# Pre-activation pair network on one core: the float16 high part of the normalised input from a second product instead of a cast

## The chip, the core and the metric

The kernel runs on one core of a Trainium2 chip. The metric is the device time of one execution in microseconds, as the median of repeated runs. The core has TensorE (PE, matmuls), VectorE (DVE), ScalarE (ACT), GpSimd (POOL) and the DMA queue of SyncE (SP), each with an instruction stream of its own. They meet through semaphores: an instruction may add to one when it is done, and an engine may wait until one has reached a value. Inputs and outputs lie in HBM, working data in SBUF (128 partitions), and matmuls write to PSUM, 8 banks of 512 float32 columns per partition.

## What is computed

x has the shape (1, 256, 256, 64). A group norm over 32 channel pairs is followed by a first layer that adds to x, then the same again with a second layer. The first layer begins with a layer norm over the channels, and that is the part the change touches:

```python
def _ln(x, w, b):
    mu = jnp.mean(x, axis=-1, keepdims=True)
    var = jnp.var(x, axis=-1, keepdims=True)
    return (x - mu) * jax.lax.rsqrt(var + EPS) * w + b
zn = _ln(z, ln_in_w, ln_in_b)
a = m * jax.nn.sigmoid(zn @ w_ag + b_ag) * (zn @ w_ap + b_ap)
b = m * jax.nn.sigmoid(zn @ w_bg + b_bg) * (zn @ w_bp + b_bp)
p = jnp.einsum('bikc,bjkc->bijc', a, b)
x = _ln(p, ln_out_w, ln_out_b) @ w_z + b_z
g = jax.nn.sigmoid(zn @ w_g + b_g)
return x * g
```

The second layer has gates, projections and a product of the same kind, with a norm over the whole tensor.

## The kernel before

All of x stays in SBUF, transposed, in the tensor XT_ALL (XT is a view of it): 64 groups of four image rows, 128 x 512 float32 each. The projections run as float16 matmuls in three terms, so each group of the normalised input is kept as a float16 high part, half(n, 0), and a float16 low part, half(n, 1), which together take the place of the group's float32 values in XT_ALL.

Stages, in order: load and transpose with the group statistics (to 60 us), the layer norm (60 to 236 us), gates and projections with the channel-wise products of the first layer (to about 500 us), the end of the first layer, then the second layer in the same way. The change lies in the layer norm.

The layer norm takes the 64 groups in four rounds of TG = 16, numbered t = 0 to 3. Two things run against each other:

- PE and ACT compute the variances, in the order of the function round_. For each group PE multiplies with a centring matrix (into banks 0 to 3), ACT writes the centred values back to XT_ALL (L844) and their squares to sq (L849), and PE adds the squares up into bank 4. Each of the two float32 matmuls of a group stands as two records.
- DVE, in normalise, turns the variances of a round into reciprocal spreads, split into three bfloat16 parts (parts3, L1232 to L1246). ACT's root (L835) is in the middle of it. Then for each group a small bfloat16 matmul of PE, spread_rstd, broadcasts the reciprocal spread to a bank, 5 or 6 in turn, DVE multiplies the centred group with that bank into one of eight slots of zn in float32 (L1258), and one group later casts the slot to float16 into half(n, 0) (L1279, in high). POOL subtracts the high part from the slot, which gives half(n, 1) (L997).

The spreads of round t-1 are put into PE's stream during the variance work of round t: from its sixth step on, two and one per step in turn (the order within a step: centring matmul, sum of the squares of the group before, spreads). A spread waits on zn_done until the product that last read its bank is done. PE runs its stream strictly in order, and so a spread that waits holds the variance work behind it. The next round's variances go to bank 4 only after DVE has read the old ones in L1232, by way of ACT, whose root comes ahead of its centring work.

The last round, t = 3, has no variance work beside it. There ACT makes the high parts (L862), DVE makes every third low part (L1274) and POOL the others.

DVE's product waits for bc_done (the spread is there) and lo_done (the slot's user of eight groups back, lo_done of n - 7, is done).

Of the kernel before, what the change touches and what calls it, by code (L numbers as in the profile page):

```python
# [37 lines left out]
GR = 4  # L38
# [19 lines left out]
TG = 16  # L58
NT = NG // TG
# [29 lines left out]
def build(nc, x, mask, w0, w1, bias0, bias1, vecs, consts, norm_consts, spread, ones3, out):  # L89
# [4 lines left out]
    ALU = mybir.AluOpType  # L94
    ACT = mybir.ActivationFunctionType
    ds = bass.ds
# [9 lines left out]
    with ctx:  # L106
# [3 lines left out]
        def sem(name):  # L110
            return ctx.enter_context(nc.semaphore(name))
# [3 lines left out]
        XT = XT_ALL[:, :].rearrange("p (r n) -> p r n", n=P)  # L115
# [16 lines left out]
        PS = ctx.enter_context(nc.psum_tensor("PS", [P, 8, BANK], f32))  # L132
# [4 lines left out]
        def half(g, i):  # L137

            return halves[:, ds(g * (2 * BANK) + i * BANK, BANK)]
# [32 lines left out]
        zn = xs.rearrange("p s r m -> p (s r m)")[:, 0:8 * BANK].rearrange("p (s n) -> p s n", s=8)  # L172
# [67 lines left out]
        hi_done = sem("hi_done")  # L240
# [13 lines left out]
        zn_done = sem("zn_done")  # L254
# [54 lines left out]
        def new_x_bank(g):  # L309

            return g % 2 + (0 if isinstance(g, int) and g >= NG - 2 else 2)
# [4 lines left out]
        def low_count(u):  # L316

            return NG - TG + sum(v not in LOWS_V for v in range(u + 1))
# [33 lines left out]
        def reached(eng, semaphore, value):  # L352

            if not isinstance(value, int) or value > 0:
                eng.wait_ge(semaphore, value)
# [136 lines left out]
        def _(pe):  # L492
            def mm(dst, lhsT, rhs, start=True, stop=True):
                return nc.tensor.matmul(dst, lhsT, rhs, start=start, stop=stop)  # L494
# [19 lines left out]
            for q in range(2):  # L514
                for h in range(2):
                    src = maskn.rearrange("p (h c q) -> p h q c", h=2, q=2)[:, h, q]
                    last = nc.tensor.transpose(PS[:, 7, (2 * q + h) * P:(2 * q + h + 1) * P], src, ident)
# [38 lines left out]
            def spread_rstd(t, u):  # L556

                if u == 0:
                    pe.wait_ge(rb_ready, t + 1)

                reached(pe, zn_done, t * TG + max(u - 1, 0))
                mm(PS[:, 5 + u % 2, :], spread_sb[:, u * P:(u + 1) * P], parts3).then_inc(bc_done, 1)


# [1 line left out]
            def round_(t):  # L566
                spread = 0
                for u in range(TG + 1):
                    if u < TG:
                        reached(pe, sq_ready, t * TG + (u - 3))  # L570
                        mm(PS[:, u % 4, :], cs, XT[:, ds(t * (TG * GR) + u * GR, GR), :].rearrange("p r n -> p (r n)")
                           ).then_inc(mm1_done, 1)
                    if u >= 1:
                        v = u - 1
                        pe.wait_ge(sq_ready, t * TG + (v + 1))
                        if v == 0:

                            reached(pe, var_ready, t + 1)
                        s0 = L_SEL + 30 - 2 * v
                        mm(PS[0:96, 4, :], NCF[:, s0:s0 + 96], sq[:, v % 2], v == 0, v == TG - 1).then_inc(mm2_done, 1)  # L580
                    if isinstance(t, int) and t == 0:
                        if u == SPREAD_LAG:
                            fold_weights()
                        if u == 2 * SPREAD_LAG:

                            small([(PS[:, 7, P:2 * P], ones, diag),
                                   (PS[:, 7, 2 * P:2 * P + 1], out_sq, ones[:, 0:1])])
                    elif SPREAD_LAG <= u < TG:
                        for _ in range(1 if (u - SPREAD_LAG) % 2 or u == TG - 1 else 2):
                            spread_rstd(t - 1, spread)  # L590
                            spread += 1
                assert spread in (0, TG)

            rounds(pe, round_, NT, 2)
            for layer in range(2):
# [113 lines left out]
                if layer == 0:  # L709
                    for u in range(TG):  # L710
                        spread_rstd(NT - 1, u)
                    pe.wait_ge(lo_done, low_count(TG - 1))
                    pe.wait_ge(lo_done_v, len(LOWS_V))
                else:

                    pe.wait_ge(biases_ready, 1)
                    for n in range(AP):
                        add_bias(0, n, False).then_inc(proj_done[1], 1)
# [3 lines left out]
                if layer == 1:  # L722
# [5 lines left out]
                    for step in range(NG + 2):  # L728
# [12 lines left out]
                        if 0 <= g < NG:  # L741
                            pe.wait_ge(o_done, g + 1)
                            reached(pe, ob_ready, g - 1)
                            for r in range(GR):
                                last = nc.tensor.transpose(PS[:, 6 + g % 2, r * P:(r + 1) * P],  # L745
                                                           x1sum[:, g % 4, r:BANK:GR], ident)
# [6 lines left out]
                for step in range(NG + 3):  # L753
                    g = step
                    if g < NG:
# [3 lines left out]
                        for r in range(GR):  # L759
                            last = nc.tensor.transpose(PS[:, 4 + g % 2, r * P:(r + 1) * P], pn[:, g % 2, r, :], ident)  # L760
# [6 lines left out]
                    if 0 <= g < NG:  # L767
# [5 lines left out]
                        for r in range(GR):  # L773
                            last = mm(bank[:, r * P:(r + 1) * P], pt[:, g % 2, r * P:(r + 1) * P], w_out,
                                      False, r == GR - 1)
                        last.then_inc(z_done, 1)
                    g = step - 3
                    if 0 <= g < NG:
# [11 lines left out]
                        for r in range(GR):  # L790
                            row = g * GR + r
                            last = nc.tensor.transpose(PS[:, new_x_bank(g), r * P:(r + 1) * P],  # L792
                                                       xb[:, row // HR % HS, row % HR, :], ident)
# [284 lines left out]
        def _(dve):  # L1078
# [17 lines left out]
            V = nc.vector  # L1096
# [132 lines left out]
            def normalise(t, last=False):  # L1229

                dve.wait_ge(mm2_done, t * TG + TG)
                V.tensor_scalar(ve[0:96, :], PS[0:96, 4, :], EPS, None, ALU.add).then_inc(var_ready, 1)  # L1232
                dve.wait_ge(std_ready, t + 2)
                r, w = rt[0:96, :], tmp[0:96, :]
                chain(t, V.reciprocal(r, sd[0:96, :]))
                chain(t, V.scalar_tensor_tensor(w, r, -0.5, r, ALU.mult, ALU.mult))
                chain(t, V.tensor_tensor(w, w, ve[0:96, :], ALU.mult))
                chain(t, V.scalar_tensor_tensor(r, w, 1.5, r, ALU.add, ALU.mult))

                reached(dve, bc_done, t * TG)  # L1240
                chain(t, V.tensor_copy(parts3[0:96, :], r))
                chain(t, V.tensor_tensor(r, r, parts3[0:96, :], ALU.subtract))
                chain(t, V.tensor_copy(parts3[32:64, :], r[32:64, :]))
                chain(t, V.tensor_copy(parts3[64:96, :], r[64:96, :]))
                chain(t, V.tensor_tensor(r[64:96, :], r[64:96, :], parts3[64:96, :], ALU.subtract))
                V.tensor_copy(parts3[64:96, :], r[64:96, :]).then_inc(rb_ready, 1)  # L1246
                for u in range(TG):
                    n = t * TG + u
                    dve.wait_ge(bc_done, n + 1)

                    if last and u >= 8:
                        if u - 8 in LOWS_V:
                            dve.wait_ge(lo_done_v, LOWS_V.index(u - 8) + 1)
                        else:
                            dve.wait_ge(lo_done, low_count(u - 8))
                    else:
                        reached(dve, lo_done, n - 7)
                    V.tensor_tensor(zn[:, u % 8], XT[:, ds(n * GR, GR), :].rearrange("p r n -> p (r n)"),  # L1258
                                    PS[:, 5 + u % 2, :], ALU.mult).then_inc(zn_done, 1)
                    if not last:  # L1260
                        if u > 0:
                            high(n - 1, (u - 1) % 8)
                    elif u - 2 in LOWS_V:
                        low(u - 2)
                if not last:
                    high(t * TG + TG - 1, (TG - 1) % 8)
                else:
                    assert LOWS_V[-1] < TG - 2

            def low(u):  # L1270

                n = NG - TG + u
                dve.wait_ge(hi_done, n + 1)
                V.tensor_tensor(half(n, 1), zn[:, u % 8], half(n, 0), ALU.subtract).then_inc(lo_done_v, 1)  # L1274

            def high(n, slot):

                dve.wait_ge(zn_done, n + 1)
                V.tensor_copy(half(n, 0), zn[:, slot]).then_inc(hi_done, 1)  # L1279

            CHAIN = 9
            made = [0]
# [1 line left out]
            def chain(t, ins):  # L1284

                made[0] += 1
                ins.then_inc(dve_chain, 1)
                dve.wait_ge(dve_chain, t * CHAIN + made[0])

            def normalise_round(t, last=False):  # L1290
                made[0] = 0
                normalise(t, last)
                assert made[0] == CHAIN
# [295 lines left out]
```

## Time and profile before

| | us |
|---|---|
| median of 3 runs | 1127.15 |
| lowest, highest | 1126.86, 1130.52 |
| profiled execution, device time | 1127.89 |
| profiled execution, span of the core | 1126.1 |
| PE, DVE, ACT, POOL busy in the span | 1005.5, 868.8, 688.3, 526.2 |

The span runs from the core's first to its last instruction; the device time has 1.8 us around it. Busy shares over the whole span hide the stages: in the layer norm the engines wait for each other in another pattern than later. Timelines give the start and the duration of an instruction, and in brackets how long its engine idled ahead of it and who ended that.

### The profile page before, as it was taken

The page shows a single profiled execution, that of the slowest core. Times are in us where ns is not written, and L with a number is a line of the kernel's source. Part 1 is how long each engine was busy: PE and PEld are TensorE (multiplying, and loading weights), DVE is VectorE, ACT ScalarE, POOL GpSimd, SP SyncE. Part 2 cuts the span into 40 slices and gives each one's busy share as a digit, 9 for nine tenths or more (in the row PEclk, how much of TensorE's full clock was granted, in tenths as well). Part 3 has the DMA queues.
Part 4 walks back from the last instruction along what each step waited for, and adds up shares of the span by engine and source line. Part 5 has one row for each costly group of instructions (what it writes and reads, how often), then busy time and mean ns, then how long its engine had stood idle before and what let it go on. Part 6 is the DMA issues. An engine that isn't in the chain of part 4 may idle for free.

```text
span 1126.1 us, 36346 instructions
## 1 busy us (share of the span) xinstructions
PE 1005.5 (89%) x14204; PEld 784.8 (70%) x14204; DVE 868.8 (77%) x1302; ACT 688.3 (61%) x1102; POOL 526.2 (47%) x447
## 2 busy tenths in 40 slices
PE   5699798579999999978999994989989898879997
PEld 5543333268898888968999994768777786645554
DVE  6817988966876868678888887866848678479997
ACT  5757565455656556565776672766847667546664
POOL 0001554586190734606777771542716437045553
PEclk9989999779999999998999996989999999989999
DMA  9800000000302112079989920003040130499995
GB/s 350 305 10 0 0 1 0 1 2 19 135 4 113 41 65 89 22 217 263 209 193 200 202 49 1 4 29 126 4 135 20 52 102 3 150 186 281 267 273 188
DMA packets 173196, 121.32 MB, mean 108 GB/s; under 512 B 69764, under 2 KB 152068, under 8 KB 173064
## 3 DMA queue, kind: packets, MB, share of 16 engines
q1 hardware_dynamic: 173064, 119.34, 39.8%
q8 instruction: 110, 1.80, 0.7%
q14 instruction: 22, 0.18, 0.1%
HBM read 68.99 MB, written 50.33 MB: 106 GB/s over the span
## 4 chain that ended last, share of the span: by engine, by line
PE 58%; DVE 16%; issue 11%; ACT 4%; DMA 4%; POOL 3%; DVEq 1%; SPq 1%; ACTq 0%; POOLq 0%
PE PS L494 53%; DVE WK L1399 4%; DMA AB<-x 3%; PE PS L760 3%; ACT WK L874 2%; PE PS L792 2%; DVE AB L1329 1%; DVE AB L1258 1%; DVE WK L1320 1%; POOL XT_ALL L997 1%; DVE AB L1325 1%; POOL AB L1058 1%; POOL AB L349 1%; DVE XT_ALL L1279 1%; DMA AB<-k_scratch 1%
## 5 line engine op out<-in xcount | busy, mean ns | idle before, releaser
L494 PE MATMUL PS<-EFF,XT_ALL 64*128 64x64 f16 (+1 forms) x10368 | 343.6, 201 | 8.7 <-POOL XT_ALL L997 3.6
L494 PEld LDWEIGHTS PS<-EFF,XT_ALL 64*128 64x128 f16 (+1 forms) x10368 | 316.4, 97 | 42.4 <-issue 16.4
L494 PE MATMUL PS<-AB 128*128 128x256 f16 (+3 forms) x1482 | 298.6, 355 | 41.8 <-POOL AB L1058 11.8
L494 PEld LDWEIGHTS PS<-AB 128*128 128x128 f16 (+3 forms) x1482 | 204.7, 140 | 133.6 <-issue 38.1
L874 ACT ACTIVATE WK<-PS,T 128x512 f32<-128x512 f32 x256 | 171.1, 683 | 94.9 <-PE PS L494 69.1
L1058 POOL TENSOR_TENSOR AB<-WK,AB 128x512 f32 x96 | 122.3, 1276 | 152.7 <-ACT AB L884 151.2
L349 POOL TENSOR_TENSOR AB<-WK,MS 128x512 f32 x96 | 130.6, 1388 | 105.6 <-DVE WK L1315 105.5
L997 POOL TENSOR_TENSOR XT_ALL<-AB,XT_ALL 128x512 f32 (+1 forms) x59 | 69.8, 1191 | 165.2 <-DVE XT_ALL L1279 154.9
L1068 POOL TENSOR_TENSOR WK<-XT_ALL 128x512 f32 (+1 forms) x64 | 73.8, 1155 | 85.3 <-PE PS L745 58.4
L1315 DVE TENSOR_TENSOR WK<-PS,WK 128x512 f32<-128x512 f32 x128 | 86.8, 689 | 31.2 <-ACT WK L874 24.9
L1320 DVE TENSOR_TENSOR WK<-PS,WK 128x512 f32<-128x512 f32 x128 | 87.3, 685 | 22.4 <-ACT WK L874 22.4
L1347 DVE BATCH_NORM_STATS2 REC<-WK 128x512 f32 x64 | 44.4, 694 | 61.6 <-ACT WK L906 61.6
L1403 DVE SCALAR_TENSOR_TENSOR WK<-WK,T 128x512 f32<-128x512 f32 x64 | 74.8, 1169 | 7.8 <-DVE WK L1399 2.0
L928 ACT ACTIVATE WK<-PS,T 128x512 f32<-128x512 f32 x64 | 49.4, 777 | 50.8 <-PE PS L494 50.8
L844 ACT ACTIVATE XT_ALL<-PS,T,CF 128x512 f32<-128x512 f32 (+1 forms) x64 | 49.7, 776 | 48.6 <-PE PS L494 48.6
L906 ACT ACTIVATE WK<-PS,T 128x512 f32<-128x512 f32 x64 | 44.0, 688 | 57.0 <-PE PS L494 56.2
L913 ACT ACTIVATE WK<-PS 128x512 f32<-128x512 f32 x64 | 41.1, 642 | 47.3 <-PE PS L494 45.6
L884 ACT ACTIVATE AB<-WK 128x512 f32 (+1 forms) x96 | 60.5, 630 | 15.4 <-DVE WK L1320 14.7
L494 PEld LDWEIGHTS PS<-EFF,WK 128*128 128x128 f32 x512 | 68.6, 195 | 1.9
L1342 DVE TENSOR_TENSOR S<-S,WK 128x512 f32<-128x512 f32 x64 | 44.6, 698 | 32.0 <-ACT WK L913 31.0
L494 PE MATMUL PS<-AB,EFF 128*128 128x512 f32 x128 | 66.7, 606 | 2.5 <-DMA AB<-k_scratch 2.5
L494 PE MATMUL PS<-EFF,WK 128*128 128x128 f32 x512 | 68.7, 278 | 0.0
(194 smaller groups left out, 1593.8 us busy)
## 6 DMA issues: line engine op xcount, KB each, us to landing
AB<-x SPq DMA_DIRECT2D x64, 512.0 KB, 7.0
p_scratch<-WK SPq DMA_DIRECT2D x32, 512.0 KB, 2.6
k_scratch<-WK SPq DMA_DIRECT2D x64, 256.0 KB, 2.1
AB<-k_scratch SPq DMA_DIRECT2D x32, 512.0 KB, 11.4
out<-AB SPq DMA_DIRECT2D x16, 1024.0 KB, 11.4
AB<-p_scratch SPq DMA_DIRECT2D x29, 512.0 KB, 7.6
AB<-p_scratch SPq DMA_DIRECT2D x2, 640.0 KB, 6.4
RAW<-w SPq DMA_DIRECT2D x2, 256.0 KB, 2.6
```

The costliest lines, as they stand in the source:

```text
L349: return eng.tensor_tensor(ab[:, :, :, ds(n4 * (4 * PR) + u * PR, PR)], sig[:, u], rows.unsqueeze(2).to_broadcast([P, 2, 2 * CHUNK, PR]), ...
L494: return nc.tensor.matmul(dst, lhsT, rhs, start=start, stop=stop)
L844: nc.scalar.activation(XT[:, ds(n * GR, GR), :].rearrange("p r n -> p (r n)"), PS[:, u % 4, :], ACT.Identity, bias=T[:, 15:16], scale=CF[: ...
L874: nc.scalar.activation(sig[:, u % 4], unit(layer, u)[:, :, 0:2 * CHUNK, :], ACT.Sigmoid, scale=T[:, 22:23] if layer == 0 else T[:, 28:29]) ...
L884: nc.scalar.activation(ab_hi[:, :, :, ds(n8 * (UB * PR) + u * PR, PR)], sig[:, u % 4], ACT.Copy).then_inc(abhi_done, 1)
L928: nc.scalar.activation(gate1[:, k % 4], PS[:, k % 4, :], ACT.Sigmoid, bias=T[:, 32:33], scale=T[:, 28:29]).then_inc(gate1_ready, 1)
L997: nc.gpsimd.tensor_tensor(half(n, 1), zn[:, u % 8], half(n, 0), ALU.subtract).then_inc(lo_done, 1)
L1058: nc.gpsimd.tensor_tensor(ab_rows(ab_lo, n4, u), sig[:, u], ab_rows(ab_hi, n4, u), ALU.subtract).then_inc(ablo_done, 1)
L1068: nc.gpsimd.tensor_tensor(x1sum[:, k % 4], half(g, 0), half(g, 1), ALU.add).then_inc(x1sum_done, 1)
L1315: V.tensor_tensor(gate, lin, gate, ALU.mult).then_inc(prod_done[0], 1)
L1320: V.tensor_tensor(gate, lin, gate, ALU.mult).then_inc(prod_done[1], 1)
L1403: V.scalar_tensor_tensor(x1sum[:, k % 4], x1sum[:, k % 4], col(24), gate1[:, k % 4], ALU.mult, ALU.add).then_inc(o_done, 1)
```

## The change

In the rounds t = 0 to 2 the helper high is gone. In its place DVE runs the product of L1258 a second time, directly after the first, with the same two inputs (the centred group in XT_ALL and the spread in PSUM) and with half(n, 0), float16, as its output; it adds to hi_done. It writes over the front half of the group that it reads. The bank of a spread is now read by two instructions, so that a later spread into it waits on hi_done instead of zn_done, except from the third spread of the last round on.

```diff
@@ spread_rstd (PE)
-                reached(pe, zn_done, t * TG + max(u - 1, 0))
+                if isinstance(t, int) and t == NT - 1 and u >= 2:
+                    pe.wait_ge(zn_done, t * TG + u - 1)
+                else:
+                    reached(pe, hi_done, t * TG + max(u - 1, 0))
                 mm(PS[:, 5 + u % 2, :], spread_sb[:, u * P:(u + 1) * P], parts3).then_inc(bc_done, 1)
@@ normalise (DVE)
                     V.tensor_tensor(zn[:, u % 8], XT[:, ds(n * GR, GR), :].rearrange("p r n -> p (r n)"),
                                     PS[:, 5 + u % 2, :], ALU.mult).then_inc(zn_done, 1)
                     if not last:
-                        if u > 0:
-                            high(n - 1, (u - 1) % 8)
+                        V.tensor_tensor(half(n, 0), XT[:, ds(n * GR, GR), :].rearrange("p r n -> p (r n)"),
+                                        PS[:, 5 + u % 2, :], ALU.mult).then_inc(hi_done, 1)
                     elif u - 2 in LOWS_V:
                         low(u - 2)
-                if not last:
-                    high(t * TG + TG - 1, (TG - 1) % 8)
-                else:
+                if last:
                     assert LOWS_V[-1] < TG - 2
-            def high(n, slot):
-
-                dve.wait_ge(zn_done, n + 1)
-                V.tensor_copy(half(n, 0), zn[:, slot]).then_inc(hi_done, 1)
```

On DVE, at the start of the groups of round 0, this stood there (AB holds parts3 and zn, PS is PSUM; line, operation, output, inputs, the semaphores waited for):

```order
L1245 TENSOR_TENSOR AB<-AB 32x512 [waits dve_chain]
L1246 CAST AB<-AB 32x512 [waits dve_chain]
L1258 TENSOR_TENSOR AB<-XT_ALL,PS 128x512 [waits bc_done] x2
L1279 CAST XT_ALL<-AB 128x512 [waits zn_done]
L1258 TENSOR_TENSOR AB<-XT_ALL,PS 128x512 [waits bc_done]
```

and at the same place stands now:

```order
L1248 TENSOR_TENSOR AB<-AB 32x512 [waits dve_chain]
L1249 CAST AB<-AB 32x512 [waits dve_chain]
L1261 TENSOR_TENSOR AB<-XT_ALL,PS 128x512 [waits bc_done]
L1264 TENSOR_TENSOR XT_ALL<-XT_ALL,PS 128x512
L1261 TENSOR_TENSOR AB<-XT_ALL,PS 128x512 [waits bc_done]
```

The high part of a group comes right behind its product and waits for nothing, where it stood behind the product of the next group.

On PE, in the variance steps of round 1 with the spreads of round 0 (96x512 is the sum of the squares, 128x512 from AB alone a spread), before:

```order
L494 MATMUL PS<-XT_ALL,AB 128x512 [waits sq_ready]
L494 MATMUL PS<-AB 96x512 [waits sq_ready]
L494 MATMUL PS<-AB 128x512 [waits zn_done] x2
L494 MATMUL PS<-XT_ALL,AB 128x512 [waits sq_ready]
L494 MATMUL PS<-AB 96x512 [waits sq_ready]
L494 MATMUL PS<-AB 128x512 [waits zn_done]
```

and now:

```order
L494 MATMUL PS<-XT_ALL,AB 128x512 [waits sq_ready]
L494 MATMUL PS<-AB 96x512 [waits sq_ready]
L494 MATMUL PS<-AB 128x512 [waits hi_done] x2
L494 MATMUL PS<-XT_ALL,AB 128x512 [waits sq_ready]
L494 MATMUL PS<-AB 96x512 [waits sq_ready]
L494 MATMUL PS<-AB 128x512 [waits hi_done]
```

The order is the same; only the semaphore that the spreads wait for differs.

## Rows read from the trace of the kernel before

**Rows 1.** Timeline of DVE, L1232: start us, us, engine, line, operation, [idle before]
```profile
95.18 0.69 DVE L1232 TENSOR_SCALAR AB<-PS 96x512 f32<-96x512 f32 x1 [3.53 <-PE PS L494]
...
132.66 0.69 DVE L1232 TENSOR_SCALAR AB<-PS 96x512 f32<-96x512 f32 x1 [0.22 <-DVE T L1141]
...
170.81 0.68 DVE L1232 TENSOR_SCALAR AB<-PS 96x512 f32<-96x512 f32 x1
...
208.50 0.68 DVE L1232 TENSOR_SCALAR AB<-PS 96x512 f32<-96x512 f32 x1
```

**Rows 2.** Timeline of DVE, products and casts of rounds 0 and 1
```profile
110.27 0.69 DVE L1258 TENSOR_TENSOR AB<-XT_ALL,PS 128x512 f32<-128x512 f32 x1 [0.73 <-PE PS L494]
...
131.35 0.14 DVE L1299 TENSOR_SCALAR T<-T 128x1 f32<-128x1 f32 x1
...
150.32 0.42 DVE L1279 CAST XT_ALL<-AB 128x512 f32 x1
150.66 0.68 DVE L1258 TENSOR_TENSOR AB<-XT_ALL,PS 128x512 f32<-128x512 f32 x1
151.25 1.13 DVE L1279 CAST XT_ALL<-AB 128x512 f32 x1
152.31 0.67 DVE L1258 TENSOR_TENSOR AB<-XT_ALL,PS 128x512 f32<-128x512 f32 x1
```

**Rows 3.** Timeline of POOL in the same stretch of round 1
```profile
150.95 1.16 POOL L997 TENSOR_TENSOR XT_ALL<-AB,XT_ALL 128x512 f32 x1 [0.59 <-DVE XT_ALL L1279]
152.59 1.16 POOL L997 TENSOR_TENSOR XT_ALL<-AB,XT_ALL 128x512 f32 x1 [0.49 <-DVE XT_ALL L1279]
```

**Rows 4.** Timeline of ACT, steps of L844 in rounds 0 and 1
```profile
99.92 0.78 ACT L844 ACTIVATE XT_ALL<-PS,T,CF 128x512 f32 x1 [0.91 <-PE PS L494]
...
109.30 0.78 ACT L844 ACTIVATE XT_ALL<-PS,T,CF 128x512 f32 x1 [0.58 <-PE PS L494]
...
113.38 0.78 ACT L844 ACTIVATE XT_ALL<-PS,T,CF 128x512 f32 x1 [0.58 <-PE PS L494]
...
115.53 0.78 ACT L844 ACTIVATE XT_ALL<-PS,T,CF 128x512 f32 x1 [0.79 <-PE PS L494]
...
117.46 0.78 ACT L844 ACTIVATE XT_ALL<-PS,T,CF 128x512 f32 x1 [0.58 <-PE PS L494]
...
126.85 0.78 ACT L844 ACTIVATE XT_ALL<-PS,T,CF 128x512 f32 x1 [0.58 <-PE PS L494]
...
139.16 0.78 ACT L844 ACTIVATE XT_ALL<-PS,T,CF 128x512 f32 x1 [2.67 <-PE PS L494]
```

**Rows 5.** Timeline of PE: variance matmuls, and one weight load (PEld) of a spread
```profile
93.97 1.10 PE L494 MATMUL PS<-AB 128*96 128x512 f32 x2 [0.59 <-ACT AB L849]
...
97.83 1.10 PE L494 MATMUL PS<-AB 128*96 128x512 f32 x2 [1.04 <-ACT AB L849]
...
109.86 0.10 PEld L494 LDWEIGHTS PS<-AB 128*128 128x128 bf16 x1 [0.33 <-issue]
...
128.26 1.10 PE L494 MATMUL PS<-AB 128*96 128x512 f32 x2 [0.47 <-ACT AB L849]
...
135.38 2.02 PE L494 MATMUL PS<-AB 128*96 128x512 f32 x2 [4.31 <-ACT AB L849]
...
173.52 2.02 PE L494 MATMUL PS<-AB 128*96 128x512 f32 x2 [3.00 <-ACT AB L849]
```

**Rows 6.** Single lines: duration ns min/median/max, first and last start us
```profile
L1258 DVE TENSOR_TENSOR AB<-XT_ALL,PS x64: 672/675/689, 106.2 to 232.0; 128x512 f32<-128x512 f32 x64
...
L1279 DVE CAST XT_ALL<-AB x48: 413/1124/1200, 107.4 to 208.2; 128x512 f32 x32, 128x512 f16<-128x512 f32 x16
...
L1403 DVE SCALAR_TENSOR_TENSOR WK<-WK,T x64: 750/1212/1599, 995.7 to 1119.1; 128x512 f32<-128x512 f32 x64
...
L1450 DVE SCALAR_TENSOR_TENSOR XT_ALL<-PS,T,XT_ALL x64: 681/742/751, 520.0 to 686.8; 128x512 f32 x48, 128x512 f16<-128x512 f32 x16
```

**Rows 7.** Busy time by stretch: bounds, length, engines' busy time, granted PE clock
```profile
135.00:138.00 3.00, 2.62 (x3) 1.07 (x4) 2.96 (x2) 1.49 (x3) 0.00 (x0) 0.57 0.00 0
```

## The prediction

> **What bounds the kernel now.** First I read the chain of waits for the stretch in which the normalised input is made, then the timelines of DVE, POOL, ACT and PE for it. Three rounds of 16 groups each lie there, t = 0, 1 and 2; the fourth round (t = 3) has another code path, which the change leaves alone. A round begins with the DVE operation of L1232, which turns the variance into what ACT takes the root of. It starts at 95.18, 132.66, 170.81 and 208.50 us [rows 1]: the rounds last 37.48, 38.15 and 37.69 us. In a round DVE first makes the reciprocal spread (one chain of ten operations), then per group a product (L1258) and a cast to float16 (L1279); POOL subtracts the cast for the low half (L997). At the same time PE and ACT compute the variances of the next 16 groups, and PE puts the broadcasts ("spreads") for DVE between those matmuls.
>
> Who is late? In the first four groups DVE waits for PE (0.73 us at 110.27 in round 0), and a cast there takes 0.42 us (150.32 in round 1). From the next group on a cast takes 1.13 us, and from there on the timeline marks no wait of DVE up to the end of the round [rows 2]: product to product is 152.31 - 150.66 = 1.65 us. In the same stretch POOL runs 1.16 us and then waits 0.49 us for the cast [rows 3], a cycle of the same 1.65 us. The rows fit one picture: a cast started while POOL works (151.25, POOL 150.95 to 152.11) ends 0.27 us after POOL, so it waits POOL out and then runs, and POOL waits for it in turn. DVE and POOL go one after the other. Their cycle is 1.16 + 0.27 + 0.2 us of handing over.
>
> PE wants a slower beat than DVE's uncontended one and a faster one than this. Read on the start of ACT's L844, which follows each PE variance step: 2.15 us for a step with two spreads and 1.93 us for one with a single spread (113.38, 115.53, 117.46) [rows 4]. Three groups per two steps is 4.08 / 3 = 1.36 us a group. At 1.65 DVE falls behind, the spreads wait for their bank, and at the end DVE has casts left when PE is long done: L1232 at 170.81 and at 208.50 follows the last cast with no idle time marked before it [rows 1]. So these rounds are bounded by DVE together with POOL, and by PE's beat if that goes away.
>
> **The change part by part.**
>
> *Cast out, second product in.* 48 casts go, of 413 (POOL idle) to 1200 ns, median 1124 [rows 6]. In come 48 products that read the same two operands as L1258, one of them from PSUM, and write float16. L1258 itself takes 672 to 689 ns in all 64 executions, most of them with POOL busy; from a product's start to the next instruction's it is 151.25 - 150.66 = 0.6 us [rows 2]. Float16 output: L1450 reads PSUM and writes float16 with 681 to 751 ns, also while POOL works [rows 6]; it is a scalar_tensor_tensor with a column scale besides, so the product is nearer to L1258. I take 0.60 us start to start, with 0.67 (L1450's) as the upper end of the likely. A pair is then 1.20 to 1.27 us in place of 1.65. A bound far above: an operation with both inputs in SBUF stretches beside POOL, L1403 to a median of 1.21 and at most 1.60 us [rows 6]. Nothing below 0.60 is seen for 512 float32 elements out of PSUM, so no gain beyond that.
>
> The Trainium skill ("VectorE: DVE Perf Modes", The perf-mode tier table) speaks against the change: a float32 tensor_copy in SBUF runs at twice the rate of a tensor_tensor with a PSUM operand. By that alone the time would not move (a rival below). The trace has both prices, 0.42 against 0.675 us, but the first only where POOL idles; beside POOL it is 1.13 against 0.675. The Trainium skill, "SBUF — State Buffer" (Who interferes with whom), names a reason: an exclusive port pair, which a copy in a 2-port mode needs and an operation with one SBUF input does not.
>
> *POOL.* 1.16 us a group with 1.20 to 1.36 on offer: it keeps up, and the slot of zn that DVE waits for was filled eight groups back.
>
> *The wait of the spreads.* Spread u now waits for hi of group u-2 in place of its product, 0.6 us later. Take a double step, with ACT's step at 0. The product of its first spread starts at 0.97 (110.27 - 109.30) [rows 2, 4], and with pairs of 1.20 the second product's pair runs from 2.17 to 3.37. The next step, a single, comes at 2.15; its product would start at 3.12 and is held by DVE to 3.37, and its hi, which starts at 3.97 and takes 0.675, is done at 4.65. The next double step comes at 4.08, and its second spread, the one that needs this bank, loads its weights 0.56 us behind that (109.86 - 109.30) [rows 4, 5], at 4.64. So it meets a bank that comes free at the same moment; with a semaphore's way in between I take 0.06 us for each of the five doubles, an estimate: 0.3 us a round.
>
> *The length of a round then.* From L1232 of a round to its 16th ACT step: in round 0 the 12th step stands at 117.46, still unhindered, and the four that follow take 2.15 + 1.93 + 2.15 + 1.93 = 8.16, giving 125.62 where the trace has 126.85 [rows 4]. That is 30.44 us after 95.18; with the 0.3 above 30.74. The last variance matmul starts 1.41 us after that step (128.26 - 126.85) [rows 4, 5] and L1232 starts 1.21 us after that (95.18 - 93.97) [rows 1, 5]. DVE's last pair begins 0.97 us after the 16th step and takes 1.20, so DVE is free 0.45 us before PE. Round 0 has six small DVE operations behind its last pair (131.35 to 132.66, 1.31 us) [rows 1, 2], so there L1232 stands at 30.74 + 0.97 + 1.20 + 1.31 = 34.22 us, against 37.48: **3.3 us**. A later round is 30.74 + 1.41 + 1.21 = 33.36 us, if PE's clock holds.
>
> *The clock.* After L1232 PE idles until ACT has the first square: 4.31 us before 135.38 and 3.00 before 173.52, and in both places the matmul pair then takes 2.02 us in place of 1.10 [rows 5], at a granted clock of 0.57 on the mean of 135 to 138 us, most of it at 1.2 in place of 2.4 GHz [rows 7]; after 1.04 us of idling (97.83) it stays up [rows 5]. ACT waits 0.91 us before its third step of round 0 (99.92) and 2.67 before that of round 1 (139.16) [rows 4], so such a fall costs 1.8 us. With the change L1232 comes at 95.18 + 34.22 = 129.4 and PE's first sum 2.65 us later (97.83 - 95.18), at 132.05. PE's last sum starts at 95.18 + 30.74 + 1.41 = 127.33, and that one and the two matmuls behind it take 2.82 us (97.83 - 1.04 - 93.97), to 130.15. It idles 1.9 us, between the two cases, and before round 2 for 1.04 us. I let round 1 keep its fall and round 2 lose it. Round 1: 38.15 - 33.36 - 1.8 = **3.0 us**; round 2: 37.69 - 33.36 = **4.3 us**.
>
> *After that.* From 208.50 on everything hangs on the chain of L1232 and moves with it; the fourth round's waits are the same for 14 of its 16 spreads, and the other two ask for a count that is reached long before. No DMA is under way there (share 0.00) [rows 7]. Nothing late is put in place of the wait removed except PE's own beat.
>
> Sum: 3.3 + 3.0 + 4.3 = 10.6 us. The profiled execution's time is 1127.89 with a span of 1126.1; the span would be 1115.5, and on the median of 1127.15 that is **1116.5 us**.
>
> **The rivals.**
>
> *Pairs a little long.* If the second product has L1450's 0.67 start to start or some more, up to 0.76 (pair 1.36, PE's beat), each of the five double steps of a round holds PE by 0.15 to 0.3 us: 3 x 5 x 0.15 to 0.3 = 2.3 to 4.5 us of the gain gone, 1118.8 to 1121. For it: PE's stream is in order, and a held spread holds the variance behind it. Against: L1258's flat duration.
>
> *Nothing.* POOL takes the bound over: with 1.16 us [rows 3] at present it would have to stretch beside the second product to the 1.65 us of the old cycle, and then DVE, which may be eight groups ahead at most, waits for it and the time is 1127. Up to 1.36 us it would cost nothing. Against it: L1258 runs beside it now and POOL's time is 1.16 us in each group.
>
> *The bare prices.* If the long casts cost the round nothing, because PE's spreads are what is late anyway, only the prices of the instructions count. A pair goes from 0.6 + 0.34 (150.66 - 150.32) = 0.94 to 1.20 us [rows 2], both under PE's 1.36, and the time stays at 1127. This is what the tier table of the Trainium skill would give. Against it: L1232 follows the last cast, not PE, in two rounds of three.
>
> *Slower.* The second product fights POOL as operations with two SBUF inputs do, at DVE in the groups from the fourth on (39 in three rounds). It decides from 1.05 us start to start, where a pair reaches 1.65. At L1403's median (1.21, so 1.13 start to start) it adds 0.08 x 39 = 3 us: 1130; at its longest (1.60, 1.52) it adds 0.47 x 39 = 18 us: 1145. For it: it writes XT_ALL, the tensor POOL also writes, and reads it in place. Against: L1258 shares both inputs, and L1450 both the PSUM source and the output tensor, and neither stretches beside POOL.
>
> *The clock goes the other way.* No fall in round 1 either: 1114.7. Falls in both rounds: 1118.3. These belong to the forecast.
>
> **How the numbers follow.** Forecast with its clock cases (1114.7 to 1118.3) 0.64; pairs a little long (1118.8 to 1121) 0.20; nothing, by POOL 0.04 and by the bare prices 0.02; slower 0.05; the rest, a gain larger than 12.5 us, 0.05. To leave out no more than 0.2 the range goes from 1113 (the clock phase after the long idle of PE at 209 to 235 us may give back another 1.5 us) to 1121. A measurement of this kernel tells about 0.3%, 3.4 us, from no change: forecast and the long-pair case are both beyond that, so faster 0.89, same 0.06, slower 0.05.
>
> **What the profile of the changed kernel would show.** L1232 at 95.2, 129.4, 164 to 165 and 198 us; the second product near 675 ns beside POOL, no group of it at 1.1 us; DVE waiting for PE in most groups again; POOL still 1.16 us but waiting a little less per group; ACT's steps at 2.15 and 1.93 to the end of a round; the PE idle before round 2 near 1 us with the clock up. I am wrong if the second product stretches beside POOL, if spreads wait for it by more than 0.1 us each, or if POOL takes over as what ends last.

## The result and the profile after

| | before | after |
|---|---|---|
| median, us | 1127.81 (1126.86 to 1130.52, 4 runs) | 1113.51 (1112.76 to 1114.72, 4 runs) |
| ratio of the two | | 0.987, 95% interval 0.985 to 0.9891 |
| span of the profiled execution | 1126.1 | 1112.9 |

The changed kernel is 14.3 us faster, where 10.6 were forecast (1116.5). The time lies in the range, near its lower end.

The timeline of DVE shows the rounds by the start of the operation that was L1232 and is L1235 now (start us, us, engine, line, operation, idle time before it):

```profile
96.44 0.69 DVE L1235 TENSOR_SCALAR AB<-PS 96x512 f32<-96x512 f32 x1 [3.52 <-PE PS L494]
...
130.37 0.69 DVE L1235 TENSOR_SCALAR AB<-PS 96x512 f32<-96x512 f32 x1 [0.22 <-DVE T L1144]
...
165.20 0.69 DVE L1235 TENSOR_SCALAR AB<-PS 96x512 f32<-96x512 f32 x1 [0.17 <-PE PS L494]
...
198.15 0.69 DVE L1235 TENSOR_SCALAR AB<-PS 96x512 f32<-96x512 f32 x1
```

The rounds last 33.93, 34.83 and 32.95 us against 37.48, 38.15 and 37.69 [rows 1], together 11.6 us less. At 165.20 DVE waits for PE's last sum, which it did not at 170.81.

Three groups of round 0 on DVE, from the same timeline:

```profile
115.60 0.69 DVE L1261 TENSOR_TENSOR AB<-XT_ALL,PS 128x512 f32<-128x512 f32 x1 [0.41 <-PE PS L494]
116.21 0.68 DVE L1264 TENSOR_TENSOR XT_ALL<-XT_ALL,PS 128x512 f16<-128x512 f32 x1
116.81 0.68 DVE L1261 TENSOR_TENSOR AB<-XT_ALL,PS 128x512 f32<-128x512 f32 x1
117.41 0.68 DVE L1264 TENSOR_TENSOR XT_ALL<-XT_ALL,PS 128x512 f16<-128x512 f32 x1
118.00 0.68 DVE L1261 TENSOR_TENSOR AB<-XT_ALL,PS 128x512 f32<-128x512 f32 x1
118.60 0.68 DVE L1264 TENSOR_TENSOR XT_ALL<-XT_ALL,PS 128x512 f16<-128x512 f32 x1
119.69 0.69 DVE L1261 TENSOR_TENSOR AB<-XT_ALL,PS 128x512 f32<-128x512 f32 x1 [0.41 <-PE PS L494]
```

and the view of single lines (duration ns min/median/max) for the second product and for POOL's subtraction:

```profile
L1264 DVE TENSOR_TENSOR XT_ALL<-XT_ALL,PS x48: 677/679/683, 108.0 to 197.4; 128x512 f32 x32, 128x512 f16<-128x512 f32 x16
...
L1000 POOL TENSOR_TENSOR XT_ALL<-AB,XT_ALL x59: 1147/1157/1602, 109.0 to 224.0; 128x512 f32 x48, 128x512 f16<-128x512 f32 x11
```

Three groups take 119.69 - 115.60 = 4.09 us: two pairs of 1.20 us, a third of 1.28 us to the end of its last product, and a wait of 0.41 us for PE. That is PE's beat of 4.08 us for three groups [rows 4]. The second product takes 677 to 683 ns in all 48 executions, where the cast took up to 1200 [rows 6]. POOL still takes its 1.16 us, but now runs three groups on end and then waits (start us, us, ...):

```profile
113.02 3.55 POOL L1000 TENSOR_TENSOR XT_ALL<-AB,XT_ALL 128x512 f32 x3 [0.53 <-DVE XT_ALL L1264]
117.09 3.62 POOL L1000 TENSOR_TENSOR XT_ALL<-AB,XT_ALL 128x512 f32 x3 [0.53 <-DVE XT_ALL L1264]
```

### The profile page after: what moved, and what is told of

Same layout as the page of the kernel before. It is cut to its first block, busy times and chain, and to the rows that moved or that the text cites. A ratio compares the mean times of both kernels' runs of the same rounds, so it can differ in the third digit from the quotient of the medians.

```text
span 1112.9 us, 36346 instructions
## 1 busy us (share of the span) xinstructions
PE 1000.7 (90%) x14204; PEld 781.9 (70%) x14204; DVE 856.2 (77%) x1302; ACT 688.1 (62%) x1102; POOL 526.7 (47%) x447
## 4 chain that ended last, share of the span: by engine, by line
PE 61%; DVE 15%; issue 10%; ACT 4%; DMA 4%; POOL 3%; DVEq 1%; SPq 1%; ACTq 0%; POOLq 0%
PE PS L494 56%; DVE WK L1395 4%; DMA AB<-x 3%; PE PS L763 2%; ACT WK L877 2%; PE PS L795 2%; DVE AB L1325 2%; DVE WK L1316 1%; POOL XT_ALL L1000 1%; DVE AB L1321 1%; POOL AB L1061 1%; POOL AB L349 1%; DMA AB<-k_scratch 1%; PE PS L508 1%; DVE XT_ALL L1446 1%
## 5 line engine op out<-in xcount | busy, mean ns | idle before, releaser
L494 PE MATMUL PS<-AB 128*128 128x256 f16 (+3 forms) x1482 | 294.1, 352 | 32.4 <-POOL AB L1061 11.8
```

## The experiments

The theory: a DVE cast that starts beside POOL's subtraction waits until that has ended, which makes a pair of 1.65 us; the pair's length against PE's beat of 1.36 us a group decides how long a round is, and nothing else in the edit matters. The rivals: the cast's place and wait, POOL as a bound of its own, a price of the cast beyond the pair, and, for the part of the gain outside the rounds, something later in the program that the change owns.

This table has all kernels with a profile, before and after among them: the three rounds, their sum, and the rest of the span (span less that sum). All columns but the last are of the one profiled execution. That is not always a typical one: the profiles of e2, e4, e5, e7 and e9 are of the fastest execution of the kernel, those of the changed kernel (row "after") and of e1 of the slowest (e5: 1126.17 against a median of 1130.0). The rounds repeat to about 0.2 us but for the two cases of round 1 after the change; the rest does not, see e9 to e11.

| kernel | round 0 | round 1 | round 2 | sum | rest | median us |
|---|---|---|---|---|---|---|
| before | 37.48 | 38.15 | 37.69 | 113.3 | 1012.8 | 1127.8 |
| before again (e10) | 37.50 | 38.07 | 37.92 | 113.5 | 1013.0 | 1128.3 (1 run) |
| after | 33.93 | 34.83 | 32.95 | 101.7 | 1011.2 | 1113.5 |
| after again (e9) | 33.93 | 33.21 | 32.95 | 100.1 | 1010.5 | 1114.1 |
| after, third (e11) | 33.92 | 34.84 | 32.95 | 101.7 | 1011.0 | 1114.5 (1 run) |
| e1, cast, short POOL | 34.00 | 33.05 | 32.81 | 99.9 | 1014.0 | 1114.4 |
| e2, product, short POOL | 33.92 | 33.20 | 32.95 | 100.1 | 1009.8 | 1113.9 |
| e3, two SBUF inputs | 41.63 | 43.47 | 42.13 | 127.2 | 1011.5 | 1141.2 |
| e4, pad of 128 | 35.13 | 34.49 | 34.28 | 103.9 | 1009.8 | 1117.1 |
| e5, pad of 384 | 38.89 | 37.87 | 37.71 | 114.5 | 1009.9 | 1130.0 |
| e6, six moved | 32.98 | 33.20 | 32.95 | 99.1 | 1012.8 | 1113.4 |
| e7, warm | 33.92 | 33.21 | 32.95 | 100.1 | 1006.8 | 1111.3 |
| e8, both | 32.98 | 33.20 | 32.95 | 99.1 | 1010.1 | 1111.0 |

### e1: the cast kept, POOL's instruction halved

```diff
@@ kernel before, POOL, rounds 0 to 2
-nc.gpsimd.tensor_tensor(half(n, 1), zn[:, u % 8], half(n, 0), ALU.subtract).then_inc(lo_done, 1)
+nc.gpsimd.tensor_tensor(XT_ALL[:, ds(n * BANK + BANK // 2, BANK // 2)], zn[:, u % 8][:, 0:BANK // 2],
+                        zn[:, u % 8][:, 0:BANK // 2], ALU.subtract).then_inc(lo_done, 1)
```

> The kernel before, cast and all, but POOL's subtraction in rounds 0 to 2 covers half the columns and writes zeros (the low part of 48 groups is left out), so POOL holds SBUF for about 0.6 instead of 1.16 us a group. Theory (the cast waits for POOL's instruction to end): a cast beside POOL ends about 0.27 us after POOL does, the pair comes to 0.6 + 0.27 + 0.2 = 1.1 to 1.2 us, under PE's beat of 1.36, and the rounds become those of the changed kernel: 33.5 to 35 us each, time 1112 to 1116. Rival 1 (what cost was the cast's place one group later and its wait on the product, not POOL): casts stay at 1.1 us, rounds at 37.5 to 38, time 1127.

Measured: 1114.4 us, ratio 0.9878 (0.9857 to 0.9899). DVE's timeline, then POOL's, in round 1, and the casts as one line:

```profile
153.17 0.68 DVE L1263 TENSOR_TENSOR AB<-XT_ALL,PS 128x512 f32<-128x512 f32 x1
153.77 0.64 DVE L1284 CAST XT_ALL<-AB 128x512 f32 x1
...
156.31 0.69 DVE L1263 TENSOR_TENSOR AB<-XT_ALL,PS 128x512 f32<-128x512 f32 x1 [0.82 <-PE PS L494]
156.91 0.42 DVE L1284 CAST XT_ALL<-AB 128x512 f32 x1
```

```profile
153.51 0.61 POOL L1001 TENSOR_TENSOR XT_ALL<-AB 128x256 f32 x1 [1.29 <-DVE XT_ALL L1284]
```

```profile
L1284 DVE CAST XT_ALL<-AB x48: 418/426/642, 107.0 to 194.2; 128x512 f32 x32, 128x512 f16<-128x512 f32 x16
```

The same cast in the same place has a median of 426 in place of 1124 ns. The one at 153.77 starts while POOL works (153.51 to 154.12) and ends at 154.41, 0.29 us after POOL: the 0.27 us of [rows 2, 3] over again, behind a shorter instruction. DVE waits for PE 0.82 us per three groups, twice what it does after the change, since a cast alone is the cheaper of the two. Two of the rounds (33.05 and 32.81 us) are a little under the 33.5 to 35 expected. The whole gain is there with the cast kept, so its place and its wait cost nothing. And the cheaper pairs gain nothing over the changed kernel: the rounds sum to 99.9 us against the 100.1 of e9.

### e2: the changed kernel, POOL's instruction halved

The edit of e1, made on the changed kernel.

> The changed kernel with the same halved POOL subtraction (the low part of 48 groups is left out). Theory (POOL is off the path once the cast is gone): rounds as in the changed kernel, 33.9, 34.8 and 33.0 us within 0.3, time 1112 to 1115. Rival 2 (POOL's 1.16 us, or its nearness to DVE's products, is part of the new bound): rounds shorter by over 0.7 us each, time under 1111.

Measured: 1113.9 us, ratio 0.9884 (0.9865 to 0.9903). Rounds 0 and 2 are those of the changed kernel to 0.01 us; round 1 is the 33.20 that the changed kernel has too when PE's clock stays up (e9). POOL's length does not count once the cast is gone.

### e3: two SBUF inputs in the cast's place

```diff
@@ kernel before, high
-V.tensor_copy(half(n, 0), zn[:, slot]).then_inc(hi_done, 1)
+V.scalar_tensor_tensor(half(n, 0), zn[:, slot], 1.0, zn[:, slot], ALU.mult, ALU.max).then_inc(hi_done, 1)
```

> The kernel before with the cast replaced, in the same place, by a scalar_tensor_tensor that takes the float32 slot of zn twice (both inputs in SBUF, the larger of x*1 and x) and writes float16. Theory A (two SBUF inputs meet POOL's reads as L1403 does): it takes 1.2 to 1.6 us beside POOL, the pair is 1.7 to 2.0 us, the rounds 38 to 43 us, time 1128 to 1142. Theory B (only a copy in the fast mode meets POOL): it takes 0.69 us, the pair is 1.2 to 1.3, time 1113 to 1117.

Measured: 1141.2 us, ratio 1.012 (1.0101 to 1.014). DVE's timeline, then POOL's:

```profile
157.13 0.67 DVE L1258 TENSOR_TENSOR AB<-XT_ALL,PS 128x512 f32<-128x512 f32 x1
157.73 1.39 DVE L1279 SCALAR_TENSOR_TENSOR XT_ALL<-AB 128x512 f32 x1
159.04 0.67 DVE L1258 TENSOR_TENSOR AB<-XT_ALL,PS 128x512 f32<-128x512 f32 x1
```

```profile
157.42 1.16 POOL L997 TENSOR_TENSOR XT_ALL<-AB,XT_ALL 128x512 f32 x1 [0.75 <-DVE XT_ALL L1279]
```

The line alone has 677 / 1387 / 1461 ns: 0.68 without POOL, 1.39 beside it. It ends 0.54 us after POOL (159.12 against 158.58), and the cycle is 1.16 + 0.75 = 1.91 us. Round 1 took 43.47 us, a little over the 38 to 43 expected. So a float16 output from DVE is not free of POOL as such. What sets the change's second product apart is that one of its inputs comes from PSUM; the first product, with a float32 output and a PSUM input, never stretched either. The Trainium skill ("SBUF — State Buffer", Who interferes with whom) says that a DVE operation in a 2-port mode contends with GpSimd for a port pair that they share, that one with two SBUF inputs contends with a GpSimd instruction that reads SBUF, and that one with at most one SBUF input, outside the 2-port modes, does not. The medians here agree: 1124 ns for the cast with the full subtraction against 426 with the halved one (e1), 1387 for two SBUF inputs (e3), and 679 for the second product.

### e4 and e5: the pair made longer without POOL

```diff
@@ changed kernel, normalise (e5; e4 has 128 in place of 384)
                     if not last:
+                        V.tensor_scalar(WK[:, (u % 4) * BANK:(u % 4) * BANK + 384], PS[:, 5 + u % 2, 0:384],
+                                        1.0, None, ALU.mult)
                         V.tensor_tensor(half(n, 0), ...
```

> The changed kernel with an extra DVE operation per group between the two products, a tensor_scalar of 128 columns from the spread's bank: the pair comes to about 1.20 + 0.20 = 1.40 us, just over PE's beat of 1.36. Theory (a pair costs only what it is over the beat, and a little for the spreads' later banks): each of the three rounds is 0.3 to 1.5 us longer than in the changed kernel, time 1114.5 to 1118. Rival (any longer pair costs in full, 0.2 x 48 = 9.6 us): time 1123.

> The changed kernel with one more DVE operation per group between the two products, a tensor_scalar of 384 columns from the spread's bank to an unused place: no cast, no meeting with POOL, but a pair of about 1.2 + 0.47 = 1.67 us, as long as before. Theory (the length of DVE's pair against PE's beat of 1.36 us is all that counts): the rounds are back at 37 to 39.5 us, time 1125 to 1131. Rival (the cast itself or its meeting with POOL costs beyond the pair's length): rounds of 34 to 36 us, time 1114 to 1119.

Measured: e4 1117.1 us, ratio 0.9909 (0.9892 to 0.9926); e5 1130.0 us, ratio 1.002 (1.0009 to 1.0032). DVE's timeline of e5, round 1:

```profile
147.26 0.68 DVE L1261 TENSOR_TENSOR AB<-XT_ALL,PS 128x512 f32<-128x512 f32 x1
147.86 0.55 DVE L1264 TENSOR_SCALAR WK<-PS 128x384 f32<-128x384 f32 x1
148.33 0.67 DVE L1266 TENSOR_TENSOR XT_ALL<-XT_ALL,PS 128x512 f32 x1
148.92 0.68 DVE L1261 TENSOR_TENSOR AB<-XT_ALL,PS 128x512 f32<-128x512 f32 x1
```

e5's pair is 148.92 - 147.26 = 1.66 us, the length it had with the cast (1.65 [rows 2]), and its rounds sum to 114.5 us against 113.3: the time is that of before to 0.2%, with no cast in it. So close a match is partly luck. The long pair also applies to the first groups, where product and cast cost 0.94 us before, and that makes round 0 longer by 1.41 us. It does so in rounds 1 and 2 as well, but there PE's clock stayed up in e5, where it fell before:

```profile
137.02 1.09 PE L494 MATMUL PS<-AB 128*96 128x512 f32 x2 [2.99 <-ACT AB L852]
```

The first product of round 1 then comes 145.60 - 134.30 = 11.30 us after the start of the round, in the kernel before 12.99 us (145.65 - 132.66):

```profile
145.65 1.29 DVE L1258 TENSOR_TENSOR AB<-XT_ALL,PS 128x512 f32<-128x512 f32 x2 [2.84 <-PE PS L494]
```

In round 2 it is 11.13 against 12.53 us. These 1.7 and 1.4 us make up for the longer first pairs. Behind the first groups the two kernels go at the same 1.65 and 1.66 us a group, which is what the theory asks for.

e4's pair is 1.40 us, 0.04 over the beat, and its rounds are longer by 1.20, 1.28 (against the 33.21 of e9) and 1.33 us, within the 0.3 to 1.5 expected. The full 0.2 x 16 = 3.2 us a round, which the rival asked for, is not there. The 1.2 to 1.3 us are more than 0.04 x 16 = 0.6 us, and PE's timeline of e4, round 0, shows why: a spread now waits openly for the second product (L1266 here), twice in the round.

```profile
110.58 0.39 PE L494 MATMUL PS<-AB 128*128 128x512 bf16 x1 [0.28 <-DVE XT_ALL L1266]
...
119.20 0.39 PE L494 MATMUL PS<-AB 128*128 128x512 bf16 x1 [0.18 <-DVE XT_ALL L1266]
```

The four steps of ACT in which the bank comes late take 2.61, 2.24, 2.51 and 2.25 us in place of 2.15, together 1.0 us, and the last pair is 0.2 us longer: that is the 1.20 us of round 0. e4 and e5 lie above the knee and e1 below it: of a pair shorter than the beat of 1.36 us nothing counts, of one longer the excess, and a little more at the spreads.

### e6, e7, e8: what is left at the seams

e6 moves the six small operations (col(26) to col(25)) from between rounds 0 and 1 to behind the last round. e7 puts matmuls into PE's idle time around the last round:

```diff
@@ changed kernel, PE, before the projection's first wait
+                    pe.wait_ge(var_ready, NT + 1)
+                    warm(38)                  # each: mm(PS[:, 4, :], w_hi[:, 0:P], w_hi[:, 0:BANK])
                     for u in range(TG):
                         spread_rstd(NT - 1, u)
+                        warm(1)
+                    warm(14)
                     pe.wait_ge(lo_done, low_count(TG - 1))
```

> The changed kernel with the six small DVE operations that stand between rounds 0 and 1 moved behind the last round, where DVE waits for POOL anyway. Theory: round 0 is then bounded by PE's last sum as the others are, 33.9 - 0.9 = 33.0 us; PE idles about 1.1 instead of 1.99 us ahead of round 1, so its clock stays up there and round 1 takes 33.0 to 33.3 in place of 34.8 us (or of 33.2 where it stayed up before): time 1110.5 to 1113. Rival (they were hidden): no change, 1113.5.

> The changed kernel with idle-time matmuls (38 before the spreads of the last round, one behind each, 14 behind the last, all into a bank that nobody reads) so that PE's clock does not fall there. Theory (the half clock from the last round into the projection costs time): spreads of 0.4 instead of 0.6 us, the first stretch of the projection 31.5 instead of 34.3 us: 2.5 to 4.5 us less, time 1109 to 1111. Rival (the spreads are held by the matmuls put between them, and the fall comes later instead): 1113 to 1116.

> Both: the six small operations moved and the idle-time matmuls in the last round. The two act in different places and should add up: 3.5 to 7 us less than the changed kernel, time 1106.5 to 1110.

Measured: e6 1113.4 us (1111.55 to 1113.88), ratio to before 0.9869 (0.985 to 0.9888); e7 1111.3 (1108.74 to 1113.81), 0.9863 (0.9838 to 0.9888); e8 1111.0 (1110.80 to 1112.07), 0.9855 (0.9837 to 0.9873). The rounds did as expected: in e6 and e8 round 0 is 32.98 us, 0.95 less. PE idles 1.04 us ahead of round 1, and its clock stayed up:

```profile
131.41 1.09 PE L494 MATMUL PS<-AB 128*96 128x512 f32 x2 [1.04 <-ACT AB L852]
```

But e6's median is that of the changed kernel (1113.5) and just outside the 1110.5 to 1113 expected, so the time does not tell the theory from its rival; the rounds do. In its profile the rest of the span is 1012.8, 1.6 us longer, and the gain is lost again there (e9 to e11 show where). In e7 the matmuls keep the clock at 1.00 (2.4 GHz), where the changed kernel runs at half of that through the spreads of the last round. Busy time by stretch (bounds, length, busy time of PE, PEld, DVE, ACT, POOL, granted clock), first e7, then the changed kernel:

```profile
210.00:222.00 12.00, 8.78 (x48) 2.61 (x49) 9.65 (x16) 7.96 (x14) 11.73 (x9) 1.00 0.00 0
222.00:230.00 8.00, 8.00 (x274) 7.49 (x267) 6.52 (x10) 4.57 (x7) 6.49 (x5) 1.00 0.02 4
```

```profile
213.00:225.00 12.00, 5.97 (x10) 0.96 (x10) 9.57 (x15) 8.49 (x14) 12.00 (x10) 0.50 0.00 0
225.00:233.00 8.00, 7.83 (x204) 7.34 (x205) 4.62 (x7) 3.31 (x5) 4.98 (x5) 0.73 0.01 2
```

The first stretch of the projection takes 32.4 instead of 34.3 us (e8: 32.5), not the 31.5 expected. e7's median just misses the 1109 to 1111 expected, and its four executions fall in two groups (1108.7 and 1109.4, 1113.3 and 1113.8) of which the profile shows the faster. e8 has the lowest median of all and the narrowest spread, but its interval overlaps that of the changed kernel (0.985 to 0.9891), so how much it beats that one by is not settled. Its expectation of 1106.5 to 1110 was missed: of the 3.5 to 7 us less than the changed kernel 1.8 came if each is held against the runs of before beside it (16.1 against 14.3 us), 2.6 by the bare medians.

### e9, e10, e11: both kernels again

> The changed kernel once more, to see what of its gain is its own. Theory (the rounds gain 11.6 us where PE's clock falls ahead of round 1 and 13.2 where it doesn't, and the rest of the kernel takes anything from 1010 to 1014 us for reasons of its own): rounds 0 and 2 at 33.9 and 33.0 us to 0.1, round 1 at 34.8 or 33.2, and a time 11.5 to 15 us under before. Rival (a steady gain of 2 us or more later in the program, which belongs to the change): rest of the span steadily 1.5 us or more under that of before.

> The kernel before once more, with a profile. Theory: rounds of 37.5, 38.2 and 37.7 us again, with PE's clock down at the start of rounds 1 and 2 (4.3 and 3.0 us of idling), and a rest of the span between 1010 and 1014 us, where the profile shown first has 1012.8.

> The changed kernel a third time, for the spread alone: the same as the run before it, with round 1 at 34.8 or 33.2 us.

Measured: e9 1114.1 us (1112.39 to 1116.4; ratio 0.9886, 0.9866 to 0.9906), e10 1128.3 and e11 1114.5 us. Round 1 of the changed kernel has both of the lengths, 34.8 twice and 33.2 once. PE's timeline at its start, first the profile shown above, then e9:

```profile
133.09 1.38 PE L494 MATMUL PS<-AB 128*96 128x512 f32 x2 [1.99 <-ACT AB L852]
134.26 1.91 PE L494 MATMUL PS<-XT_ALL,AB 128*128 x2
```

```profile
131.97 1.09 PE L494 MATMUL PS<-AB 128*96 128x512 f32 x2 [1.99 <-ACT AB L852]
```

The same idle time of 1.99 us, once with a fall behind it and once without; in e1, e2, e4 and e7 (2.06, 1.99, 2.18 and 1.98 us) there was none.

The rest of the span is 1011.2, 1010.5 and 1011.0 in three profiles of the changed kernel and 1012.8 and 1013.0 in two of before, 1.6 to 2.5 us less, as the rival had it. It comes apart into three pieces. From the start of the span to the first round it is 95.2 and 96.5 us before, 96.4, 95.3 and 95.9 after: scatter, in one kernel as in the other. The second piece is a stretch of float16 matmuls in the second layer, which the chain of waits has as one entry (start us, us), first in the changed kernel, then in e10:

```profile
739.45 21.94 PE PS L494 x192
```

```profile
751.57 23.47 PE PS L494 x192
```

In the profile of before shown first it took 24.73 us. All that is left, from the last round's L1232 or L1235 to the end without this stretch, is 892.9 and 893.1 us before and 892.8, 893.3 and 893.1 after, the same. So what the profiles gain outside the rounds, they gain in this one stretch, 1.5 to 2.8 us, and it goes with PE's clock: 0.94 in the 33 us up to and just past its start in the kernel before (720.5 to 753.5 us), 1.00 in the same stretch of the changed kernel (710.15 to 743.15 us).

That the edit owns this is not shown. The stretch is short (21.93 or 21.94 us) in the changed kernel three times and in e2, e4, e5 and e7, but also in e3, which has neither second product nor cast; it is long in before, e10 and e1 (24.68), but also in e6 and e8 (23.54 both), which have the second product. Nor does the place in time decide it, as two pairs show, first e6 and e2, then e5 beside the 751.57 of e10:

```profile
736.23 23.54 PE PS L494 x192
```

```profile
736.29 21.93 PE PS L494 x192
```

```profile
752.02 21.94 PE PS L494 x192
```

From 736 to 745 us the granted clock is 0.81 in e6 and 1.00 in e2. What lets it fall in one and not in the other stays open. It can differ between executions of one kernel as well: the spans of the executions without a profile reach from 1123.9 to 1128.3 us for the kernel before and from 1110.6 to 1114.3 us for the changed one, more than the rounds and the start of the span differ in the profiles.

## Why the prediction was right, and where it was short

- **Cast blocked by POOL, pair of 1.65 us.** Right. e1 and e3 show both ends of the wait, e5 that a pair of that length without a cast gives the same pace, 1.66 us a group.
- **The second product at 0.60 us start to start.** Right: 0.60, duration 677 to 683 ns beside POOL. The rivals of longer pairs and of a fight with POOL would have been right for another choice of operand: e3 is the slower rival, at 1.91 us a pair and 1141 us.
- **POOL.** Right in that it keeps up at 1.16 us. The wait per group was told vaguely; it is 0.53 us once in three groups.
- **The spreads' later banks, 0.3 us a round.** Wrong: the term was reckoned from the weight load, and what counts is the matmul behind it. Here the sum lost most of 0.9 us. From L1235 to the 16th step of ACT round 0 takes 126.87 - 96.44 = 30.43 us, as in the reckoning without the allowance (30.44). The list of waits for the three rounds says why:

```profile
PEld PS L494 <- DVE XT_ALL L1264: 11.9, 27, 0.6
```

The weight loads wait for the second product 27 times, but no such line stands there for the matmuls: the load comes while the matmul before it still runs, and its wait is hidden. In rounds 1 and 2 two double steps each are 0.07 to 0.08 us late (146.18 to 148.41 is 2.23 us), 0.15 us a round. The sign of being wrong that the prediction named, spreads that wait "by more than 0.1 us each", thus came true of the loads, up to 0.6 us, and not of the matmuls.
- **Round 0: 3.3 us forecast, 3.55 measured. Round 1: 3.0 with the fall, 3.3 measured; 4.9 in e9 without it. Round 2: 4.3 forecast, 4.7 measured.** Most of each difference is the term above; the fall also costs less than the 1.8 us put, 34.83 - 33.21 = 1.6 us. The idle time before round 1 was put at 1.9 us and is 1.99; before round 2 at 1.04, as measured. To put the fall's chance in the middle was right, as the three profiles show.
- **After that.** "Moves with it" held for the last round: it is 27.0 us from its start to the first matmul of the projection before and after (235.51 - 208.50 and 225.17 - 198.15). The step that failed is that nothing changes later: the stretch in the second layer is 1.5 to 2.8 us shorter, which the forecast did not have and which the runs do not tie to the edit. With it the account closes: 11.6 to 13.2 us in the rounds, by the two cases of round 1, and 1.5 to 2.8 later are 13.1 to 16.0, around the 14.3 measured. So most of the gain was forecast for the right reason; the lower end of the range was drawn for a gain between the last round and the projection, and that did not come.
- **"DVE waiting for PE in most groups again."** Wrong: it waits in one of three, because PE sends the spreads in the pattern two, one.

## What to carry to other kernels

If a cheap DVE copy runs beside GpSimd, look at its duration in that stretch and not at its price: here 0.42 us became 1.13, and the "dearer" product with one operand in PSUM, flat at 0.68, was the faster way. Work out the beat of the engine that feeds it first: of a shorter or longer step only what lies above that beat changes the time, here 1.36 us a group. Above it, the engine falls behind and the whole stretch pays; below it, the next saving is elsewhere.

## What the runs showed of the hardware that was not expected

- A DVE operation with two inputs from SBUF took longer beside POOL than the copy did, 1.39 against 1.13 us (e3), and ended 0.54 us after POOL, the copy 0.27 us. Away from POOL they take 0.68 and 0.42 us. That fits an operation that waits POOL out and then does nearly all of its work; it was not tested further.
- The length of PE's idle time alone did not tell whether the clock falls. After 1.98 to 2.18 us of idling ahead of round 1 it fell in two of seven profiles (the changed kernel and e11; not e1, e2, e4, e7, e9). After 2.99 to 3.00 us it fell in the kernel before and in e10, not in e5. After 4.3 us (before, e10) and after 4.6 and 5.9 us (e3) it fell each time, and after 1.04 us in none, ahead of round 2 in nine profiles and ahead of round 1 in e6 and e8.
- PE's weight loads waited up to 0.6 us for a semaphore (27 of them, 11.9 us in total) while no step of the rounds came more than 0.08 us late.
- One stretch of the second layer took 21.9, 23.5 or 24.7 us in kernels that are the same there, with PE's clock down in the long ones. It alone is worth 0.25% of the time, as much as some of the edits tried here.
